# Four codes of x to a 32-bit word through the transposes, the experts chosen from token 0, and new orders of work

## The reference, cut to what matters

```python
# x (2, 512, 1024), ctx (2, 1024, 1024), all float32
q1 = fake_quant(layernorm(x), scale1, zp1)    # (clip(round(v/s + z), 0, 255) - z) * s
q2 = fake_quant(ctx, scale2, zp2)
x  = x + matmul(q1, q2)
h  = layernorm(x)
# the ratio needs |h| of all 512 tokens of a batch; vision_len = 153
ratio  = mean|h[:, 153:]| / (mean|h[:, :153]| + 1e-8)
scores = softmax(concat(h, ratio) @ gate_w + gate_b)      # 3 experts
top_val, top_idx = top_k(scores, 2); top_val /= sum + 1e-8
out_e  = act_e(h @ w1[e] + b1[e]) @ w2[e] + b2[e]         # tanh, gelu, silu
# the two experts of a batch are those that its token 0 chose;
# each token weights them with its own two top values
x = x + sum_i top_val[..., i] * out_[top_idx[:, 0, i]]
```

## Time and profile before

| | us |
|---|---|
| median of 3 runs | 405.59 (405.22 to 408.02) |
| the profiled execution, its own time | 405.39 |
| its span, first to last instruction | 403.6 |
| PE busy | 388.8 (96%) |
| DVE busy | 329.3 (82%) |
| ACT busy | 196.2 (49%) |
| POOL busy | 57.5 (14%) |

### The profile page before, as it was taken

How to read it: one execution, slowest core, us unless ns; L and a number is a source line. 1 busy time by engine, 2 the same in 40 slices (tenths; PEclk the granted TensorE clock), 3 DMA queues, 4 the chain that set the end, 5 groups by cost and what they waited for, 6 DMA issues and landing times.

```text
span 403.6 us, 5336 instructions
## 1 busy us (share of the span) xinstructions
PE 388.8 (96%) x1932; PEld 306.9 (76%) x1932; DVE 329.3 (82%) x512; ACT 196.2 (49%) x254; POOL 57.5 (14%) x78
## 2 busy tenths in 40 slices
PE   2998979999999999999999999999999999999996
PEld 2435736888888888888888888888888888888885
DVE  8799876488999788897899996596998865949983
ACT  3578554174347633661826455343476333425720
POOL 8748400000000003482100004000000000000000
PEclk9999999999999999999999999999999999999999
DMA  8993039523006586000000499600045870000112
GB/s 313 412 408 120 2 121 373 186 76 133 2 0 192 175 286 233 2 0 2 0 2 0 133 367 378 218 0 0 2 159 206 251 263 8 2 0 1 54 52 104
DMA packets 23325, 52.82 MB, mean 131 GB/s; under 512 B 1760, under 2 KB 1792, under 8 KB 23296
## 3 DMA queue, kind: packets, MB, share of 16 engines
q1 hardware_dynamic: 22592, 50.34, 35.0%
q0 software_dynamic: 640, 2.10, 1.5%
q10 hardware_dynamic: 64, 0.02, 0.0%
HBM read 48.26 MB, written 4.19 MB: 130 GB/s over the span
## 4 chain that ended last, share of the span: by engine, by line
PE 94%; DVE 3%; ACT 1%; DMA 1%; issue 0%; POOL 0%; POOLq 0%; DVEq 0%; ACTq 0%
PE ps L1577 43%; PE ps L1549 38%; PE ps L1343 7%; PE ps L1389 2%; PE ps L1375 2%; DMA xres<-in_x_dram 1%; PE ps L1352 1%; DVE bn L788 1%; ACT q1T L569 1%; PE ps L1410 1%; DVE xres L859 0%; PE ps L1275 0%; ACT q L526 0%; PE ps L1331 0%; PE ps L1316 0%
## 5 line engine op out<-in xcount | busy, mean ns | idle before, releaser
L634 ACT ACTIVATE w_hi<-raw 128x1024 fp32r<-128x1024 f32 x88 | 88.5, 1053 | 44.7 <-DVE raw L985 22.5
L954 DVE TENSOR_TENSOR w_lo<-raw,w_hi 128x1024 fp32r<-128x1024 f32 x88 | 103.3, 1217 | 2.2 <-ACT w_hi L634 1.9
L1577 PE MATMUL ps<-hT_hi,w_hi 128*128 128x512 f32 x256 | 99.9, 390 | 0.0
L1577 PE MATMUL ps<-hT_lo,w_hi 128*128 128x512 f32 x256 | 99.6, 389 | 0.0
L1577 PE MATMUL ps<-hT_hi,w_lo 128*128 128x512 f32 x256 | 99.6, 389 | 0.0
L1549 PE MATMUL ps<-w_hi,a_hi 128*128 128x512 f32 x224 | 87.6, 391 | 0.0
L1549 PE MATMUL ps<-w_hi,a_lo 128*128 128x512 f32 x224 | 87.2, 389 | 0.0
L1549 PE MATMUL ps<-w_lo,a_hi 128*128 128x512 f32 x224 | 87.2, 389 | 0.0
L722 ACT ACTIVATE act_f<-ps,b1T 128x512 f32<-128x512 f32 x32 | 22.0, 689 | 103.6 <-PE ps L1577 103.6
L1577 PEld LDWEIGHTS ps<-hT_hi,w_hi 128*128 128x128 f32 x256 | 48.1, 188 | 10.1 <-issue 0.2
L1577 PEld LDWEIGHTS ps<-hT_hi,w_lo 128*128 128x128 f32 x256 | 48.1, 188 | 10.0
(11 more groups left out here) (153 smaller groups left out, 375.9 us busy)
## 6 DMA issues: line engine op xcount, KB each, us to landing
raw<-in_L_ffn_w_dram SPq DMA_DIRECT2D x64, 512.0 KB, 5.5
raw<-in_ctx_dram SPq DMA_DIRECT2D x16, 512.0 KB, 11.6
xres<-in_x_dram SPq DMA_DIRECT2D x8, 512.0 KB, 9.6
b2row<-in_L_ffn_b_dram SPq DMA_DIRECT2D x4, 512.0 KB, 6.6
out_dram<-xres POOLq DMA_DIRECT2D x8, 256.0 KB, 8.0
out_dram<-xres SPq DMA_DIRECT2D x8, 256.0 KB, 2.0
small<-in_L_xattn_x_scale_dram ACTq DMA_DIRECT2D x2, 0.0 KB
small<-in_L_xattn_x_zp_dram ACTq DMA_DIRECT2D x2, 0.0 KB
```

The lines of the kernel that those rows point to most:

```text
L634: nc.scalar.activation(w_hi[n % SLOTS][:, 2 * c:2 * c + 2, :], region(q)[:, 2 * c:2 * c + 2, :], ACT.Copy).then_inc(w_hi_ready, 1)
L954: V.tensor_tensor(w_lo[n % SLOTS][:, 2 * c:2 * c + 2, :], region(n % QUARTERS)[:, 2 * c:2 * c + 2, :], w_hi[n % SLOTS][:, 2 * c:2 * c + 2, ...
L1577: last = T.matmul(ps[:, G1_BANK + f % 2, :], w[q % SLOTS][:, k % TT, fs], h[:, k, :], start=n == 0, stop=n == 3 * KT - 1)
```

## The change

- The codes of x are packed: `q1` holds 1024 bytes a tile, read as 256 words of 32 bits, so `transpose_q1(i)` is two float32 transposes in place of eight in float16. `load_q1T` reads bytes (with a step of four bytes) from PSUM. The rows of ctx are spread over the chunks in the matching order (row 512h + 4p + j of a batch is partition p of chunk 4h + j). `fill(0)` is gone.
- Experts are chosen from token 0 alone: `token_logits(b)` is 16 matmuls of one column of h with the gate weights (8 columns), `token_scores` (DVE) reads them, and `choose_experts` works on the raw scores, without waiting for all tokens' scores and the exponential; it needs the ratio still.
- The four `gate_product`s of a batch become one `gate_products(b)`, 16 matmuls that stream 512 tokens. `gate_turn` is four transposes. The bias b1 is turned beside the gate weights at the start.
- The orders of all engines are new: ctx chunks 0 and 1 are loaded ahead of x tiles 2 and 3; `quant_x(0)` moves from ACT to POOL, and `quant_ctx(2)` stands ahead of `quant_x(1)` on ACT; in p = 1 the choice of experts stands ahead of `result(1, 1)` on DVE.

Who does what, and the loads:

```diff
-CTX_ORDER = {"act": [5, 8, 10, 11, 15, 14],
-             "dve": [2, 4],
-             "pool": [0, 1, 3, 6, 7, 9, 12, 13]}
-Q1_ORDER = {"act": [0, 1, 3, 4],
-            "dve": [2, 7],
-            "pool": [5, 6]}
-Q1T_ORDER = {"act": [0, 1, 2, 5, 4, 7],
-             "dve": [3, 6]}
+CTX_ORDER = {"act": [2, 3, 6, 8, 11, 12, 15],
+             "dve": [4, 5],
+             "pool": [0, 1, 7, 9, 10, 13, 14]}
+Q1_ORDER = {"act": [1, 2, 5, 4],
+            "dve": [3],
+            "pool": [0, 6, 7]}
+Q1T_ORDER = {"act": [1, 3, 4, 5, 7],
+             "dve": [0, 2, 6]}
...
-    ctx_v = ctx_in.rearrange("b (k p) n -> (b k) p n", p=P)
+    ctx_v = ctx_in.rearrange("b (h p j) n -> b h j p n", h=2, j=4)
...
+            words = ps[:, Q1T_BANK[i], 0:WORDS]
+            return words.bitcast(U8).rearrange("p (h s j) -> p h j s", h=2, j=4)
...
             load_x(0)
             load_x(1)
+            load_ctx(0)
+            load_ctx(1)
             load_x(2)
             load_x(3)
-            load_ctx(0)
-            load_ctx(1)
...
                     sp.wait_ge(b2_used, TT * p)
+                if p == TOP_K:
+                    sp.wait_ge(logit_ps, B)
```

POOL's list, then ACT's, at the start:

```diff
             x_rstd(0, 1)
+            fill(7)
             x_rstd(1, 1)
-            fill(7)
+            quant_ctx(0)
+            quant_x(0)
             fill(8)
-            quant_ctx(0)
             quant_ctx(1)
...
-            quant_x(0)
+            quant_ctx(2)
             quant_x(1)
-            load_q1T(0)
+            quant_ctx(3)
             load_q1T(1)
-            quant_ctx(5)
-            quant_x(3)
-            load_q1T(2)
+            quant_x(2)
+            quant_ctx(6)
+            load_q1T(3)
             col_term(0)
             row_term(0)
```

DVE's list at the start, and in p = 1:

```diff
             x_constant()
+            x_offset()
             ctx_constants()
             q1_scales(0, 1)
-            q1_scales(1, 1)
-            x_offset()
             term_constants()
             x_stats(2)
-            quant_ctx(2)
+            q1_scales(1, 1)
             x_stats(3)
+            load_q1T(0)
             quant_ctx(4)
...
                 if p == 1:
+                    token_scores(1)
                     h_lo(1, 2)
                 t1_sum(p)
+                if p == 1:
+                    ratio_sums(1)
+                    router_bias(1)
+                    choose_experts(1)
                 result(p, 1)
-                if p == 1:
-                    router_bias(1)
                 w_lo_quarter(q + 7)
```

PE's transposes and gate products, and its list in p = 1:

```diff
-                bank = ps[:, Q1T_BANK[i], :].bitcast(F16)
-                for k in range(KT):
-                    last = T.transpose(bank[:, k * P:(k + 1) * P], q1[:, i % 2, k * P:(k + 1) * P], ident_b[:])
+                for h in range(2):
+                    last = T.transpose(ps[:, Q1T_BANK[i], h * P:(h + 1) * P],
+                                       q1[:, i % 2, h * P:(h + 1) * P], ident[:])
...
-                        last = T.matmul(ps[0:8, LOGIT_BANK, tok], gw_parts[:, k, :], h[:, k, tok],
+                        last = T.matmul(ps[0:1, TOKEN_BANK, 0:8], h[:, k, 0:1], gw_parts[:, k, :],
...
+                        last = T.matmul(ps[0:8, LOGIT_BANK[b], :], gw_parts[:, k, :], h[:, k, :],
...
                             if (i, j) == (0, 1):
+                                token_logits(1)
+                                sum_abs(1)
                                 transpose_h(1, 2)
-                                gate_product(1, 0)
-                                sum_abs(1)
-                            elif (i, j) == (1, 1):
-                                gate_product(1, 1)
                             elif (i, j) == (2, 1):
                                 transpose_h(1, 3)
-                                gate_product(1, 2)
                             elif (i, j) == (3, 1):
-                                gate_product(1, 3)
+                                gate_products(1)
```

More of the change, by code:

```diff
@@ L485, in _ @@
             quant_ctx(9)
-            quant_x(5)
+            quant_ctx(10)
             h_power(0)
@@ L489, in _ @@
             h_tile(0)
-            quant_ctx(12)
             quant_ctx(13)
+            x_rstd(6, 2)
             h_power(1)
+            quant_ctx(14)
             h_offset(1)
-            h_tile(1)
+            quant_x(6)
+            quant_x(7)
             h_power(2)
@@ L682, in _ @@
             quant_ctx(8)
+            quant_x(5)
             quant_x(4)
-            quant_ctx(10)
             quant_ctx(11)
+            quant_ctx(12)
             sum_h(0, 0)
             split_h(0, 0)
-            load_bias()
+            load_q1T(4)
+            quant_ctx(15)
+            h_tile(1)
+            sum_h(0, 1)
+            split_h(0, 1)
             load_q1T(5)
-            sum_h(0, 1)
-            load_q1T(4)
-            split_h(0, 1)
             sum_h(0, 2)
-            quant_ctx(15)
             split_h(0, 2)
-            quant_ctx(14)
             sum_h(0, 3)
+            load_q1T(7)
             split_h(0, 3)
-            gate_logits(0)
-            load_q1T(7)
-            gate_exp(0)
+            col_term(1)
             row_term(1)
-            col_term(1)
             w_hi_chunk(0, 0)
@@ L1119, in _ @@
             x_constant()
+            x_offset()
             ctx_constants()
             q1_scales(0, 1)
[L1122 to L1123 removed]
             term_constants()
             x_stats(2)
[L1126 removed]
+            q1_scales(1, 1)
             x_stats(3)
+            load_q1T(0)
             quant_ctx(4)
+            q1_scales(2, 2)
+            quant_ctx(5)
+            quant_x(3)
             gate_weights()
[L1130 to L1132 removed]
+            load_q1T(2)
             x_stats(4)
@@ L1138, in _ @@
             attn_add(0, 0)
+            x_stats(6)
             h_stats(0)
+            x_stats(7)
             attn_add(0, 1)
+            h_stats(1)
             attn_add(0, 2)
-            h_stats(1)
+            h_lo(0, 0)
+            q1_scales(6, 2)
+            h_stats(2)
+            token_scores(0)
             attn_add(0, 3)
-            h_lo(0, 0)
-            h_stats(2)
+            h_lo(0, 1)
             h_stats(3)
-            h_lo(0, 1)
-            x_stats(6)
-            x_stats(7)
+            load_q1T(6)
             h_lo(0, 2)
-            q1_scales(6, 2)
-            quant_x(7)
             tokens_abs(0)
+            ratio_sums(0)
+            router_bias(0)
             h_lo(0, 3)
-            load_q1T(6)
-            router_bias(0)
-            choose_scores(0)
             choose_experts(0)
-            gate_values(0)
+            split_col_term(1)
             split_row_term(1)
-            split_col_term(1)
             attn_add(1, 0)
             attn_add(1, 1)
+            attn_add(1, 2)
             w_lo_chunk(0, 0)
@@ L1407, in gate_turn @@
                 pe.wait_ge(logitT_ready, b + 1)
-                pe.wait_ge(ratio_read, b + 1)
+                if b:
+                    pe.wait_ge(ratio_read, b + 1)
                 for t in range(TT):
-                    last = T.matmul(ps[:, TURN_BANK[b], 4 * t:4 * t + 4], lgT[:, t * P:(t + 1) * P], pick_logit[:],
-                                    start=True, stop=True)
+                    last = T.transpose(ps[:, TURN_BANK[b], 8 * t:8 * t + 8], lgT[b][:, t * P:(t + 1) * P],
+                                       ident[0:8, 0:8])
                 last.then_inc(logit_ps, 1)
@@ L1472, in _ @@
             add_terms(0, 2)
+            codes_product(0, 3, 2)
             codes_product(0, 3, 3)
@@ L1516, in _ @@
             column_sums(1, 6)
+            row_sums(1)
+            codes_product(1, 2, 0)
+            codes_product(1, 2, 1)
             codes_product(1, 2, 2)
```

238 lines of the change are left out of this document (121 added, 117 removed).

## The result

| | before | after |
|---|---|---|
| median, us (lowest to highest, 4 runs each) | 405.71 (405.22 to 408.02) | 411.39 (409.83 to 413.66) |
| the profiled execution: own time, span | 405.39, 403.6 | 411.5, 409.8 |

The ratio is 1.0134 (1.0108 to 1.0159): slower by 1.3%. The four executions of the changed kernel had a mean granted clock of 0.995, 0.996, 0.996 (411.5, 411.28 and 413.66 us) and 1.0 (409.83 us); the profiled one is the first.

What follows compares the result with a forecast made beforehand. It took PE, busy 96% and holding 94% of the chain, to bound the kernel. Span 403.6 + 1.5 before G1 + 2.7 in p = 1 = 407.8, plus 1.8 outside: 409.6, called 409.5; range 404 to 412.3.

Steps and rivals of the forecast that it cites:

- Part 1, the landing of c2: Start: c2, one place before c3 in the queue, lands at 12.5; first product at 15.1, 3.4 us later.
- Part 1, the slow stretch: Start: PE idles, then its first products run slowly; costs 1.5 us, from none to 2.8.
- Rival A: Start: late first product without slow products, clock loss nil to 0.5; 408.0 to 408.5 us; chance 0.14.
- the 1.25 "back": Start: 18 matmuls took 5.28 against 4.0 us, waiting for codes; with chunks ready, 1.25 us returns.
- Part 1, the byte read: load_q1T on DVE, reading bytes without the doubled rate, takes 1.1 us; costs nothing at tile 0, up to 0.1 otherwise.
- Part 2: PE's work up to G1: fewer transposes, wide gate products, token_logits added at 0.95; net -1.1 us.
- Part 3: Waits up to G1: 3.5 us waited, some 3.5 before too; with the start, G1 at 66.05, +1.5 us (-1.5 to +3.5).
- Rival C: Batch 1, before G1: none of the 3.5 us is waited, clock loss nil; 404.6 us, at best 402.1; chance 0.12.
- rival D: Start: slow products over 5.6 us, or POOL and DVE delay each other; batch 0 ends after 36.5; 411 to 413; chance 0.20.
- Part 4: p = 1: DVE's steps ahead of result(1, 1) make PE wait 2.1 at transpose_h(1, 3); +2.7 us in all (+0.2 to +3.7).
- Rival B: p = 1: late start but no wait, as DVE's small steps fit; 407 us; chance 0.12.
- If DVE's steps hide: p = 1, lower bound: DVE's added steps cost PE no wait, work alone counts; +0.2 us.

Runs made afterwards that it cites:

- e2: Changed kernel with 44 small matmuls between transpose_q1(0) and transpose_q1(1), keeping PE busy in its wait at the start: 410.27 us, ratio 1.0121.
- e7: Changed kernel with whole (contiguous) rows in each ctx chunk again, as before: 411.56 us, ratio 1.0137.
- e4: Kernel before with the rows of ctx spread over the chunks: 406.2 us, ratio 1.0007.
- e6: e5 with five moves in the engines' orders meant to close the waits in batch 1: 410.59 us, ratio 1.0097.
- e3: Changed kernel with the x tiles first again: quant_x(0), quant_x(1) and both load_q1T lead on ACT, POOL and DVE orders matching: 409.16 us, ratio 1.0079.
- e1: Changed kernel with ratio, router_bias and choose_experts of p = 1 behind h_lo(1, 3) on DVE, no longer ahead of result(1, 1): 408.28 us, ratio 1.0056.
- e10: Kernel before with turn_gate_weights moved behind the first three products on PE: 407.33 us, ratio 1.0036.
- e12: e11 with x tiles 2 and 3 loaded ahead of ctx chunks 0 and 1 again: 406.82 us, ratio 1.0025.
- e5: Changed kernel with the moves of e1 and e3 both made: 406.95 us, ratio 1.0012.
- e11: e5 with turn_gate_weights moved behind the first three products on PE: 407.64 us, ratio 1.0045.
- e9: Changed kernel with 32 small matmuls ahead of transpose_h(1, 3), filling PE's wait in p = 1: 412.06 us, ratio 1.0136.

## Why the prediction was right, point by point

It said 409.5 with a range of 404.0 to 412.3, slower by over 1% in 0.42 of cases; measured 411.39, slower by 1.3%. The likeliest class, within 1% (0.51), was not what came, and 411.39 lies outside the forecast's own 408.5 to 410.8: the width of the range holds it. The two places and their signs were right; their sizes were under. Of the marks that were to show it, the first products at 600 ns and the wait in p = 1 came; the first product, the end of batch 0 (37.05 for 34 to 36), G1 (67.55 for 65 to 67) and product 3 did not.

- **Part 1, the landing of c2: the step that was mis-sized.** Counted by places in the queue it was to land at 12.5; it landed at 13.76. Then ACT's two steps took what was forecast (13.79 to 16.17 against 2.45). The two transposes took 0.69, not 0.25; kept busy in e2, PE had done them in 0.44. First product 16.90 against 15.1: 1.8 late. The 1.3 per place came from one execution with whole rows at 393 to 404 GB/s, and this one ran at 306 to 325. The stride of ctx rows, put at "nothing, or some tenths", goes with 0.7 of the 1.26 (c2 at 13.10 in e7's profile, one execution); the rest is there with whole rows too. In the medians the stride costs nothing (e4, e7).
- **Part 1, the slow stretch.** Forecast 1.5 (0 to 2.8); 14 products took 4.79 against 3.13, 1.65, and e2 took that away by keeping PE busy: shown. Rival A falls. But the 1.25 "back" was read wrongly: in the kernel before, too, the first four of the 18 products took 585 to 631 ns each and stand 0.4 apart, until 13.57, where dense ones stand 0.22 apart. So some 0.8 of the 1.25 was this same slowness and not a wait for codes, and the change made it longer (14 products 1.65 over the dense price) instead of removing it. The sum holds, as it takes one and adds the other.
- **Part 1, the byte read.** 1.24 on DVE against the 1.1 I took and 0.75 for float16; the Trainium skill ("VectorE: DVE Perf Modes", section "What auto-detection actually checks") asks for 16-bit tensors of step one for the doubled rate, and the prediction's estimate without it was 1.1 to 1.2. The row lies close above it and agrees that the doubled rate is lost. On ACT it cost nothing (1.09). Off the path, as said.
- **Part 2.** Four wide gate products took 3.71 (3.65 forecast), `gate_turn` 0.34 (0.5). `token_logits` took 0.6 at most, from 41.45 to 42.06, and 15 of its 16 matmuls start 0.03 apart; I took 0.95, the upper bound, and the truth lay in the middle of what I had given. The reason for the choice, that small matmuls aren't bound by columns, was wrong between 128 columns (0.06 apart in the kernel before) and 8.
- **Part 3.** From the end of batch 0 (37.05) to G1 it took 30.5, forecast 31.05. The waits there are 0.9, 0.7, 0.7 and 0.5: 2.9 against 3.5. `transpose_q1(5)` waited 0.9 and the products behind it 0.7, where I had 1.9 at the first; `transpose_q1(6)` and `h_lo(0, 3)` came as forecast (0.5 and 0.7); the 0.5 at `add_terms(1, 0)` is not there. Rival C, which needed them closed, falls. e6 shows what trying to close them did. Batch 0 ended at 37.05, past the 36.5 that I had given as rival D's mark, and the median lies in D's 411 to 413; but it was c2's landing that did it, and the fall of the clock in p = 1, not POOL and DVE in each other's way.
- **Part 4.** The wait at `transpose_h(1, 3)` was forecast at 2.1 and is 1.9, with the same cause; DVE's added work is 0.4 + 2.8 = 3.1 against 3.25. Rival B falls. That the wait came so near is in part luck: counted from G1, PE came 1.6 earlier (0.95 forecast), and DVE's result only 2.2 later (3.25 forecast), since DVE began that stretch 0.9 ahead. Product 3 stands 148.61 behind G1 of p = 0, before 148.55: 0.1 later, not 0.5, though the slow tile is in it, since `token_logits` was cheap and stands there in place of three gate products. Without more, p = 1 would have cost 1.8 (174.48 - 172.68, e3) and not 2.7. What was missing is the **fall of the clock behind the wait**, 1.3 more in most executions. The two errors nearly cancel: 3.1 in place of 2.7.
- **If DVE's steps hide** I gave +0.2 as the lower bound of p = 1; e1, in which they do, is at -0.66. `token_logits` (0.4 to 0.6 for 0.95) explains about half of the 0.9 between; the rest is not resolved.

**The sum** of the profile: 3.0 for 1.5, and 3.1 for 2.7. Of the 1.9 missed, 1.5 is the start (1.8 at the first product, some of it given back by `token_logits`) and 0.4 is p = 1, where an overestimate of 0.9 hides most of the missing 1.3. The one execution without the fall took 409.83, close to the 409.5 forecast. It has no trace, but with the profiles' errors of 1.5 at the start and 0.9 the other way in p = 1 that nearness is in part luck.

What stays open: why the slower loads with spread rows cost no time in the medians; why the clock falls behind the wait in some executions and not in others; and why e10 to e12 lose 0.2 to 0.5%.

## What to carry to other kernels

When an order is changed at the start of a kernel, ask of the first tile that the bound engine needs which transfer is put ahead of it on each engine that touches it: the start with one chunk ahead of `quant_x(1)` on ACT cost 1 to 2 us (e3). Steps of 0.15 us on one element add up: 19 of them ahead of the one DVE step that frees a bank for PE cost 3 us with the fall of the clock behind the wait, and the same steps behind it nothing. A short wait of PE can cost more than its length, in slow matmuls behind it; an edit that closes one wait is to be walked through every engine, for e6 closed one and opened a larger one. And where some executions of a kernel have a fall of the clock and others not, the fall is to be taken out of the difference before it is put down to an edit: it is about half of what e3 seemed to give back.

## What the runs showed of the hardware

- Behind a wait of 1.9 us PE's granted clock read 0.58 and 0.67 in this profile (0.51 and 0.76 in e2's), in other executions 1.00 behind the same wait (e3, e7). By G1 to G1 of two profiles it costs 1.3 us (175.80 against 174.48). By their mean clock ten of the sixteen executions with this wait have it (after, e2, e3, e7), none of the 31 without the wait (e1, e5, e11, e12), and four of e6's five, whose profile shows it behind a wait of 1.96 at another place. The clock was 1.00 through the wait itself and fell once PE worked again.
- At the start the granted clock reads 1.00 throughout, while products take 608 to 634 ns each and later 379. There only the durations show the slow stretch; in p = 1 the record does. The Trainium skill's page "TensorE: Matmul & The Clock Gate", section "What you observe", tells of such a rise: slow at first, full speed once it works steadily. The durations here agree (634, then 379 ns).
- Sixteen matmuls with one column of weights and 8 columns of tokens start 0.03 us apart; float32-type ones with 128 by 128 columns 0.11 (e9).
- From 6 to 9 us the loads of 512 KB ran at 325 to 345 GB/s in ten profiles with ctx rows 16 KB apart, and at 363 to 404 in four with whole rows; from 9 to 12 us both reach over 400 in most profiles. No median shows a difference (e4: 1.0007, 0.9994 to 1.002).
